# Mask of the second layer added on GpSimd, one copy moved to VectorE, casts of x moved into two gaps

## What is computed

```python
# layer 0: 6 heads of 64
q, k, v = heads(x @ Wq + bq), heads(x @ Wk + bk), heads(x @ Wv + bv)
probs   = softmax(q @ k.T / sqrt(64) + where(adj, 0, -9e15))
x       = layernorm(x + (concat(probs @ v) @ Wf + bf))
# layer 1: 12 heads of 32
h    = einsum('bnd,ade->bane', x, W)
th   = tanh(h)
attn = leaky_relu(th @ w_src + (th @ w_dst).T, 0.2)
attn = softmax(where(adj, attn, -999.0))
f    = elu(attn @ h + b)
gate = sigmoid(x @ H_w.T + H_b)
x    = layernorm(x + gate * f + (1 - gate) * x)
```

## Time and profile before

| | |
|---|---|
| median of 3 runs | 1189.36 us (1188.29 to 1189.74) |
| profiled execution | 1188.84 us |
| its span | 1187.0 us |
| granted clock of PE, mean | 0.988 |
| PE busy | 1109.9 us (94%) |
| DVE busy | 954.3 us (80%) |
| ACT busy | 945.2 us (80%) |
| POOL busy | 543.9 us (46%) |

### The profile page before, as it was taken

One profiled execution on the slowest core, in us unless ns is written; L12 is line 12 of the kernel. 1 busy time (PEld: TensorE's weight loads), 2 busy tenths in 40 slices (PEclk: granted clock), 3 DMA queues, 4 the chain that ended last, 5 costly groups with the idle time before them and its releaser, 6 DMA issues.

```text
span 1187.0 us, 25718 instructions
## 1 busy us (share of the span) xinstructions
PE 1109.9 (94%) x8428; PEld 902.9 (76%) x8428; DVE 954.3 (80%) x1958; ACT 945.2 (80%) x3447; POOL 543.9 (46%) x717
## 2 busy tenths in 40 slices
PE   6889999999999999999999999999999999997873
PEld 5667887878787787878778788877878877786652
DVE  5457888888888888888888887888888788888875
ACT  3248888888888888888888888888888888878875
POOL 0454544364454435445444544544454454444332
PEclk9899999999999999999999999999999999999997
DMA  9101001020100101010010101002010100100000
GB/s 257 54 2 54 15 25 57 8 68 15 61 15 18 65 8 68 15 60 15 15 63 12 68 15 61 15 8 68 14 68 15 62 15 8 41 15 15 15 14 21
DMA packets 25894, 44.67 MB, mean 38 GB/s; under 512 B 2462, under 2 KB 23714, under 8 KB 25762
## 3 DMA queue, kind: packets, MB, share of 16 engines
q1 hardware_dynamic: 23234, 41.91, 10.4%
q10 hardware_dynamic: 2496, 1.12, 0.5%
q0 software_dynamic: 32, 0.00, 0.0%
HBM read 30.43 MB, written 12.58 MB: 36 GB/s over the span
## 4 chain that ended last, share of the span: by engine, by line
PE 59%; ACT 23%; issue 8%; POOL 5%; DVE 3%; DMA 1%; ACTq 0%; POOLq 0%; DVEq 0%
ACT z L588 15%; PE ps_b L255 15%; PE ps_a L255 12%; PE ps_d L255 9%; PE ps_s L364 4%; ACT p1T L598 3%; PE ps_s L356 3%; PE ps_c L474 3%; POOL xT_lo L921 3%; PE ps_d L464 3%; PE ps_d L452 3%; PE ps_d L448 3%; PE ps_c L482 2%; ACT gate L664 2%; PE ps_b L411 1%
## 5 line engine op out<-in xcount | busy, mean ns | idle before, releaser
L588 ACT ACTIVATE z<-z,s 128x128 f32<-128x128 f32 x768 | 298.8, 402 | 0.5 <-DVE s L798 0.5
L958 POOL TENSOR_SCALAR s<-s 128x1 f32<-128x1 f32 x128 | 28.6, 224 | 311.8 <-DVE s L892 287.2
L973 POOL TENSOR_TENSOR p<-p,s 128x768 f32<-128x768 f32 x64 | 94.3, 1473 | 147.3 <-DVE s L804 147.3
L615 ACT ACTIVATE p<-ps_s,s 128x128 f32<-128x128 f32 x384 | 135.5, 372 | 29.4 <-DVE s L776 29.0
L588 ACT ACTIVATION_READ_ACCUMULATOR z<-z,s 128x1 f32 x768 | 154.4, 201 | 0.0
L464 PE MATMUL ps_d<-ident,z 128*128 128x128 f32 x768 | 120.0, 279 | 18.4 <-ACT z L588 8.9
L908 DVE SCALAR_TENSOR_TENSOR z<-ps_d,z 128x512 f32<-128x512 f32 x192 | 119.2, 676 | 6.3 <-ACT z L685 6.3
L981 POOL TENSOR_TENSOR thw<-th,w_sd 128x768 f32<-128x768 f32 x64 | 117.7, 1839 | 8.7 <-ACT th L636 8.5
L464 PEld LDWEIGHTS ps_d<-ident,z 128*128 128x128 f32 x768 | 90.7, 141 | 33.0 <-ACT gate L664 18.2
L598 ACT ACTIVATE p1T<-ps_d 128x512 f32<-128x512 f32 x192 | 113.4, 591 | 0.7 <-PE ps_d L464 0.7
L921 POOL TENSOR_TENSOR xT_lo<-x_cols,xT_hi 128x768 fp32r<-128x768 f32 x30 | 54.0, 1821 | 112.8 <-ACT xT_hi L555 112.8
(11 more groups left out here) (157 smaller groups left out, 3536.1 us busy)
## 6 DMA issues: line engine op xcount, KB each, us to landing
x_cols<-in_xT_dram SPq DMA_DIRECT2D x16, 768.0 KB, 6.4
xb<-in_x_dram SPq DMA_DIRECT2D x16, 768.0 KB, 4.9
out_dram<-y SPq DMA_DIRECT2D x64, 192.0 KB, 1.8
z<-in_L_gnn_Wq_dram SPq DMA_DIRECT2D x1, 576.0 KB, 6.3
p1T<-in_L_gnn_Wk_dram SPq DMA_DIRECT2D x1, 576.0 KB, 8.2
qT<-in_L_gnn_Wv_dram SPq DMA_DIRECT2D x1, 576.0 KB, 10.6
kT<-in_L_gnn_Wf_dram SPq DMA_DIRECT2D x1, 576.0 KB, 12.8
z<-in_L_gnn_W_dram SPq DMA_DIRECT2D x1, 576.0 KB, 11.6
```

The costliest lines, as they stand in the source:

```text
L588: done = act.activation(z[:, a, :], z[:, a, :], ACT.Exp, bias=neg1[:, a:a + 1], accum_out=sum1[:, a:a + 1])
L615: last = act.activation(p0[:, o, i, :], ps_s[:, o, i * N:(i + 1) * N], ACT.Exp, bias=neg0[:, k:k + 1], accum_out=sum0[:, k:k + 1])
L973: pool.tensor_tensor(p0[:].rearrange("p o i n -> p (o i) n"), p0[:].rearrange("p o i n -> p (o i) n"), inv0.unsqueeze(2).broadcast_to([P, ...
```

## The change

1. **The second layer's mask.** The three mask matmuls (L448) and the 2^100 identity go. The mask is kept as 0 or -2^53 in bf16, the scores' mask matmul uses the plain bf16 identity, and the 2^53 identity goes too. POOL adds the mask to `z` in three instructions of 128x512 (`z_mask`), each after the DVE instruction that wrote that part; DVE's maxima wait for them (`zm_ready`).
2. **POOL's order.** `z_mask` stands first in a step, behind the normalisation of `y` and ahead of p0. The normalisation of `x1` moves from the end of its step to the next step, behind `thw`; the mask's quarters and the small constants of round 1 go with it; then come `xb` and `x_lo`, which were straight behind `thw`, and the normalisation of `y` last.
3. **The first copy of `p1T`** leaves ACT and becomes a DVE copy between the split of `sd` and `cols_R`.
4. **The casts of x** (`x_hi`) on ACT in the fourth step: the first half moves ahead of `fe`, behind the evacuation of v's first quarter, the second ahead of the p0T copy, behind the evacuation of v's third.

```diff
             def logits(t):
...
-                m = mask[:, t, :].unsqueeze(1) if isinstance(t, int) else mask[:, bass.ds(t, 1), :]
+                pe.wait_ge(S["rows_ready"], t + 1)
+                pe.wait_ge(S["cols_ready"], t + 1)
                 for q in range(3):
...
-                    pe.matmul(heads, ident_100[:], m.broadcast_to([P, 4, N]), start=True, stop=False)
-                    if q == 0:
-                        pe.wait_ge(S["rows_ready"], t + 1)
-                        pe.wait_ge(S["cols_ready"], t + 1)
-                    last = pe.matmul(heads, rows_L[:, q, :], cols_R[:], start=False, stop=True)
+                    last = pe.matmul(heads, rows_L[:, q, :], cols_R[:], start=True, stop=True)
@@ ACT, in a step
                     elif qkv:
                         evacuate_v(0)
+                    if qkv and n + 1 < NG and j == 3:
+                        x_hi(g + 1, 0)
...
                     if qkv and j == 3:
                         evacuate_v(2)
+                    if qkv and n + 1 < NG and j == 3:
+                        x_hi(g + 1, 1)
...
-                    if tail:
-                        turned_p1(tl - 1, 0)
...
-                    if qkv and n + 1 < NG and j == 3:
-                        x_hi(g + 1, 0)
-                        x_hi(g + 1, 1)
@@ DVE
-                dve.tensor_scalar(ident_53[:], ident[:], 2.0 ** 53, None, ALU.mult).then_inc(S["consts_ready"], 1)
-                dve.tensor_scalar(ident_100[:], ident[:], 2.0 ** 100, None, ALU.mult).then_inc(S["consts_ready"], 1)
...
+                def turned_p1(t, q):
+                    dve.wait_ge(S["p1_turned"], 3 * t + q + 1)
+                    if due(t):
+                        dve.wait_ge(S["ph_made"], t)
+                    dve.tensor_copy(p1T[:, 4 * q:4 * q + 4, :], ps_d[:, q, :].rearrange("p (a n) -> p a n", a=4)
+                                    ).then_inc(S[f"p1T_{q}"], 1)
...
-                        dve.wait_ge(S["z_ready"], 3 * (tt + 1))
+                        dve.wait_ge(S["zm_ready"], 3 * tt + 2)
...
+                        dve.wait_ge(S["zm_ready"], 3 * (tt + 1))
                         dve.tensor_reduce(neg1[:, 8:12], z[:, 8:12, :], AX_X, ALU.max, negate=True
...
                         dve.tensor_copy(sd3[:, :, 2, :], sd_rest[:, 1, :, :]).then_inc(S["sd3_ready"], 1)
+                    if tail:
+                        turned_p1(tt, 0)
@@ POOL
-                pool.tensor_scalar(mask[:, quarter, :], adj_u8[:, quarter, :], 1.0, -1.0, ALU.mult, ALU.add
+                pool.tensor_scalar(mask[:, quarter, :], adj_u8[:, quarter, :], 2.0 ** 53, -(2.0 ** 53), ALU.mult, ALU.add
...
+            def z_mask(t):
+                for q in range(3):
+                    pool.wait_ge(S["z_ready"], 3 * t + q + 1)
+                    pool.tensor_tensor(z[:, 4 * q:4 * q + 4, :], z[:, 4 * q:4 * q + 4, :],
+                                       mask[:, t, :].unsqueeze(1).broadcast_to([P, 4, N]), ALU.add
+                                       ).then_inc(S["zm_ready"], 1)
...
+                    if tail:
+                        z_mask(tl - 1)
...
+                    if 0 <= ta - 1 < B:
+                        first_norm(ta - 1)
+                    if ta == 0:
+                        moved_constants()
+                    if 0 <= ta - 1 < 3:
+                        mask_quarter(ta)
+                    if qkv and j in (1, 2) and n > 0:
+                        xb_with_bias(g, par, slice(2 * j - 2, 2 * j))
...
                     if has_tail(n, j, 2):
...
+                        second_norm(tl - 2)
```

More of the change, by code:

```diff
@@ L70, in build_program @@
         ident_b = sb("ident_b", [P, P], BF16)
-        ident_53 = sb("ident_53", [P, P], BF16)
-        ident_100 = sb("ident_100", [P, P], BF16)
         choose = sb("choose", [P, 7])
@@ L150, in build_program @@
             x1_turned x1_hi x1_lo h_made h_ready th_ready gate_made gate_ready thw_ready
-            sd_ready split_small sd3_ready sd_turned rows_ready cols_ready logits_ready relu_ready z_ready neg1_ready
+            sd_ready split_small sd3_ready sd_turned rows_ready cols_ready logits_ready relu_ready z_ready zm_ready neg1_ready
             exp1_ready p1_turned p1T_0 p1T_1 p1T_2 ph_made fT_ready f_turned inv1_ready f_ready minus_one_ready b1_ready
@@ L342, in scores_mask @@
                 if t == 0:
-                    pe.wait_ge(S["consts_ready"], 3)
+                    pe.wait_ge(S["consts_ready"], 1)
                     pe.wait_ge(S["bf_ready"], 1)
                 for o in range(2):
-                    pe.matmul(ps_s[:, o, 0:C * N].rearrange("p (i n) -> p i n", i=C), ident_53[:],
+                    pe.matmul(ps_s[:, o, 0:C * N].rearrange("p (i n) -> p i n", i=C), ident_b[:],
                               mask[:, t, :].unsqueeze(1).broadcast_to([P, C, N]), start=True, stop=False)
@@ L963, in normalise, with second_norm, first_norm @@
                 pool.tensor_scalar(out_ap, r, nm, rs, ALU.add, ALU.mult).then_inc(S[ready], 1)
+            def z_mask(t):
[4 more added lines that the diff above has]
+                                       ).then_inc(S["zm_ready"], 1)
+            def second_norm(t):
+                pool.wait_ge(S["mv1_ready"], 2 * t + 2)
+                if t >= 2:
+                    pool.wait_ge(S[f"y_stored_{t % 2}"], 16 * (t // 2))
+                normalise(r1[:], mv1, ve1, rs1, nm1, EPS / 4, y[:, t % 2, :], "ln1_small", 3 * t, "y_ready")
+            def first_norm(t):
+                pool.wait_ge(S["mv0_ready"], 2 * t + 2)
+                if due(t - 7):
+                    pool.wait_ge(S["r1_ready"], t - 7)
+                normalise(r0[:], mv0, ve0, rs0, nm0, EPS, x1[:, t // G % 2, t % G, :], "ln0_small", 3 * t, "x1_ready")
             def iteration(g, par, n):
@@ L968, in iteration @@
                     ta, tl = G * (g - 1) + j, G * (g - 1) + j - LAG
-                    tt = tl - 1
                     gat, tail = has_gat(n, j), has_tail(n, j)
+                    if tail:
+                        z_mask(tl - 1)
                     if att:
@@ L985, in iteration @@
                         x_lo(g + 1, 1)
-                    if qkv and j in (1, 2) and n > 0:
-                        xb_with_bias(g, par, slice(2 * j - 2, 2 * j))
                     if n == 0 and j == 3:
@@ L991, in iteration @@
                     if has_tail(n, j, 2):
-                        t2 = tl - 2
-                        pool.wait_ge(S["mv1_ready"], apart(pool, 2 * t2 + 2))
-                        stored = 16 * (2 * (g - 1) + (j - LAG - 2) // 2)
-                        if due(stored):
-                            pool.wait_ge(S[f"y_stored_{(j - LAG) % 2}"], apart(pool, stored))
-                        normalise(r1[:], mv1, ve1, rs1, nm1, EPS / 4, y[:, (j - LAG) % 2, :], "ln1_small", 3 * t2, "y_ready")
-                    if att:
-                        pool.wait_ge(S["mv0_ready"], apart(pool, 2 * ta + 2))
-                        if due(ta - 7):
-                            pool.wait_ge(S["r1_ready"], apart(pool, ta - 7))
-                        normalise(r0[:], mv0, ve0, rs0, nm0, EPS, x1[:, 1 - par, j, :], "ln0_small", 3 * ta, "x1_ready")
-                    if n == 1 and j == 0:
-                        moved_constants()
-                    if n == 1 and j < 3:
-                        mask_quarter(j + 1)
+                        second_norm(tl - 2)
             pipeline(pool, iteration)
```

## The result

The changed kernel takes **1221.6 us** (median of 4 runs, 1218.93 to 1223.47) against 1188.82 of the kernel before beside it (4 runs, 1188.12 to 1189.74): a ratio of 1.0274, 95% interval 1.0253 to 1.0295. Forecast: 1208, range 1190 to 1230.

What follows compares the result with a forecast made beforehand. The prediction took PE to bound the second and third steps. First steps -18.9, second and third +18.2, fourth +18.7 and ends +1.0 gave +19.0 on 1188.84, so 1207.8, forecast as 1208 us, range 1190 to 1230.

Steps and rivals of the forecast that it cites:

- The hold: DVE's split beside POOL's xb or xT_lo stands until POOL's instruction ends: second and third steps 17.24, fourth 20.44 us.
- Rivals 1: In DVE's split, small instructions aren't held by POOL: second and third steps 15.98, in all 1144 us; chance 0.18.
- 3 (half a hold): POOL's next instruction lets DVE in earlier, each step losing half the charge: 1179, up to 1195 us; chance 0.05.
- The masks' price: Each mask addition on POOL was taken as 1.23 us, between 0.98 and 1.84.
- Rival 2: Mask additions on POOL end after DVE asks for them, at 1.84 us each: 1250 us; chance 0.05.
- the cover: POOL's mask additions end before DVE's maxima need them, hidden up to about 1.5 us each.
- The first step: With the casts of x moved, PE's 0.25 wait and late relus go: 17.32 to 15.97 us, -1.35.
- PE bounds them: In the kernel before, PE, busy 16.46 of 16.59 us, limits the second and third steps.
- The 15.98 without holds: Second and third steps if nothing is held: 16.59 less DVE's 0.61 wait for PE's p0 transposes.
- ACT gives up a copy per step, which is worth nothing where DVE leads: Moving p1T's first copy from ACT to DVE brings no gain where DVE leads.
- The ends: Start -1.0, round 1 +3.5, last three steps -1.5, round 16 unchanged: +1.0 us in all.
- the main case: The split is held and the masks are hidden: 1208 us, bounds 1196 to 1222, chance 0.72.

Runs made afterwards that it cites:

- e1: The changed kernel with POOL waiting until DVE has split the sums before it makes xb and xT_lo: 1166.2 us.
- e8: The changed kernel with xb and the two xT_lo directly behind thw, ahead of x1's normalisation, nothing waiting for the split: 1154.6 us.
- e6: The changed kernel with p1T's copy on ACT, the casts of x where they were, and POOL's earlier order behind the mask additions: 1273.0 us.
- e3: The kernel before with only the casts of x moved: 1173.7 us, ratio 0.9861.
- e7: The kernel before with only p1T's first copy moved to DVE, behind the split: 1172.9 us, ratio 0.9868.
- e5: The changed kernel with spare PE matmuls before the split sums' transposes, only where full rounds and round 1 cover them: 1217.3 us.

## Why the prediction was right

- **The hold.** The deciding step held: a DVE cast within SBUF stands until POOL's long instruction is over, with 24 columns as with 128. It had been read from the first 36 us, and gave 0.65 for the second and third steps (0.72 measured) and 1.44 for the fourth (1.55). e1 and e8 show it the other way round: without the overlap the cost is gone. Rivals 1 (small instructions pass) and 3 (half a hold) fall with it.
- **The masks' price.** 1.16 us each, against 1.23 taken and bounds of 0.98 to 1.84; hidden in the full rounds (0.9 us of waiting at L798 in the whole run). Rival 2 falls. That the cover depends on POOL's new order and the casts of x together is shown by e6; the text had the cover, not how much hung on it.
- **The first step**: 15.97 forecast, 16.03 measured. The prediction put all of the 1.35 down to the casts of x; alone they give 0.65 (e3), and the rest comes only together with the other parts.
- **"PE bounds them"**, said of the kernel before, was wrong in part: ACT's copy was on the path (e7). The 15.98 without holds came out (16.03 in e8), but partly by luck: the prediction gave the whole fall to the mask matmuls, and the copy alone brings 16.57 to 16.25 (e7), so they can't have the whole of it. That "ACT gives up a copy per step, which is worth nothing where DVE leads" was 16 us out for the copy alone; for the changed kernel, where DVE leads, no run takes the copy back by itself.
- **The ends** were the term that missed: +1.0 forecast, +8.6 measured. The start gave 2.5 instead of 1.0. Round 1 cost 7.0 instead of 3.5, and round 16 with what follows +4.1 instead of -1.5. The sum took every PE instruction at its full rate and had no term for the granted clock. With the idle time filled (e5), round 1 is 62.8, +1.7, its third and fourth steps +2.3 and +1.8 (forecast +2.5 and +1.8), and no first step of rounds 3 to 15 is late. Round 16, where "nothing changes" was said, has 2.3 us more at clocks of 0.81 and 0.90; e5, which has no spare matmuls there, has these clocks too (17.65, 16.51 and 17.65 us). For what lies behind the last L776 nothing was tried, and its part (+1.8, where some -1.5 had been forecast) stays open: it has the lower clock (0.75 against 0.85) and, at L798, the one wait for a mask (0.9 us); and the spans behind the last L776 scatter from 61.4 to 68.3 between kernels.

1208 was thus 13.6 us low: 4.2 from holds a little dearer (2.3 in the second and third steps, 1.9 in the fourth), 3.9 from first steps, 7.6 from the ends, less 1.9 because the profiled execution (1223.47) lies that much above the median, and 0.2 of rounding. The ends had been given a bound of 2 and were 7.6 out; 1221.6 lies at the very top of the main case's own bounds, 1196 to 1222, and that it lies within them is partly luck.

## What to carry to other kernels

An idle stretch on GpSimd isn't free if VectorE works within SBUF beside it: place GpSimd instructions of many columns where VectorE reads PSUM (the same work in another order is 1151.1 us here, instead of 1221.6). When TensorE gets a new wait, add a term for its clock behind it. Read the chain of waits beside the busy shares: a TensorE that is busy 16.46 of 16.59 us was waiting behind a copy on ScalarE.
